# A graph network kernel: batch-norm moments gathered inside the SpMM, in six chunks instead of five

## The reference

```python
def _sage_mean(h, src, dst, W_self, W_neigh, b):
    msg_sum = jax.ops.segment_sum(h[src], dst, num_segments=N_NODES)
    deg = jax.ops.segment_sum(jnp.ones_like(dst, jnp.float32), dst, num_segments=N_NODES)
    h_neigh = msg_sum / jnp.maximum(deg, 1.0)[:, None]
    return h @ W_self.T + h_neigh @ W_neigh.T + b

def _bn(h, gamma, beta):
    mu = jnp.mean(h, axis=0)
    var = jnp.mean(jnp.square(h - mu), axis=0)
    return (h - mu) * jax.lax.rsqrt(var + EPS) * gamma + beta
```

## Time and profile before

| | |
|---|---|
| median of 3 runs | 2182.11 us (2176.29 to 2182.74) |
| the profiled execution | 2189.64 us |
| its span, first to last instruction | 2187.5 us |
| mean granted TensorE clock, share of full speed | 0.923 |
| PE busy | 1743.2 us, 80% |
| DVE busy | 1493.0 us, 68% |
| ACT busy | 1128.8 us, 52% |
| POOL busy | 905.5 us, 41% |

### The profile page before, as it was taken

The page is one execution under the profiler, slowest core; times in us unless marked ns, Lnnn a source line. Parts: engine busy times, 40 slices in busy tenths (PEclk is TensorE's granted clock), DMA queues, the critical chain, the costliest instruction groups (busy, mean ns, idle before and its releaser), DMA issues. The chain is left out here.

```text
span 2187.5 us, 36919 instructions
## 1 busy us (share of the span) xinstructions
PE 1743.2 (80%) x9939; PEld 887.8 (41%) x9940; DVE 1493.0 (68%) x4029; ACT 1128.8 (52%) x2234; POOL 905.5 (41%) x833
## 2 busy tenths in 40 slices
PE   2777776882688878888887888779998998999776
PEld 0222222551344434444443444465535544553444
DVE  6999997434456556566555665478887887888554
ACT  5777776112333333333333333348886886888311
POOL 1000000005666666666666666325553554555300
PEclk9999999996899999898999998879999999999877
DMA  6000000102111111111111111230000000000000
GB/s 174 0 0 0 0 0 15 58 13 53 31 31 29 30 29 30 33 29 30 30 30 30 29 30 30 47 76 1 1 0 1 1 1 1 1 1 1 15 1 15
DMA packets 29632, 50.73 MB, mean 23 GB/s; under 512 B 12820, under 2 KB 13826, under 8 KB 29054
## 3 DMA queue, kind: packets, MB, share of 16 engines
q0 software_dynamic: 17664, 18.12, 4.8%
q1 hardware_dynamic: 11890, 31.59, 4.7%
HBM read 36.58 MB, written 7.39 MB: 20 GB/s over the span
## 5 line engine op out<-in xcount | busy, mean ns | idle before, releaser
L821 POOL DMA_INDIRECT adj<-h_table,l_idx x544 | 557.3, 1024 | 318.9 <-issue 150.2
L1011 DVE TENSOR_SCALAR adj<-adj,node_key 125x1024 f16<-125x1024 f16 x825 | 372.8, 495 | 357.6 <-PE psum L956 159.7
L956 PE MATMUL psum<-adj,x_sb 125*128 125x512 f16 x1650 | 438.7, 407 | 149.1 <-DVE adj L1011 131.0
L1569 POOL TENSOR_TENSOR gat_ring<-gat_ring,adj 125x750 f32<-125x750 f32 (+2 forms) x225 | 311.0, 1384 | 267.1 <-ACT gat_ring L1623 265.0
L1464 DVE SCALAR_TENSOR_TENSOR gat_ring<-x_sb,gat_node,psum 125x750 f32<-125x750 f32 (+2 forms) x375 | 317.9, 861 | 62.1 <-PE psum L1700 26.3
L884 ACT ACTIVATE l_z<-psum 128x320 f32<-128x320 f32 x204 | 89.1, 437 | 478.9 <-remote 250.9
L956 PEld LDWEIGHTS psum<-adj,x_sb 125*128 125x128 f16 x1650 | 161.4, 103 | 359.3 <-DVE adj L1011 172.2
L387 PE MATMUL psum<-col_hot,src_hot 128*128 128x500 bf16 x808 | 206.2, 377 | 110.4 <-DVE src_hot L316 89.8
L1697 PE MATMUL psum<-gat_ring,gat_hx 125*65 125x500 f32 (+1 forms) x500 | 244.2, 578 | 17.3 <-DVE gat_ring L1475 9.5
L313 DVE TENSOR_SCALAR col_hot<-iota_h,c_tab 128x500 bf16<-128x500 f16 x808 | 227.7, 346 | 25.4 <-PE psum L387 20.8
L1620 ACT ACTIVATE gat_ring<-gat_ring,gat_node 125x750 f32<-125x750 f32 (+2 forms) x225 | 182.2, 810 | 61.2 <-DVE gat_ring L1464 59.4
(11 more groups left out here) (243 smaller groups left out, 2177.5 us busy)
## 6 DMA issues: line engine op xcount, KB each, us to landing
adj<-h_table,l_idx POOLq DMA_INDIRECT x544
adj<-key_table SPq DMA_DIRECT2D x33, 250.0 KB
adj<-adj SPq DMA_DIRECT2D x3, 1662.5 KB
adj_saved<-adj SPq DMA_DIRECT2D x1, 3840.3 KB
adj<-adj_saved SPq DMA_DIRECT2D x5, 688.2 KB
x_sb<-in_x SPq DMA_DIRECT2D x1, 781.2 KB
x_saved<-x_sb SPq DMA_DIRECT2D x1, 781.2 KB
out<-x_sb SPq DMA_DIRECT2D x5, 156.2 KB
```

Source lines behind the costliest of these rows:

```text
L821: pool.indirect_dma_start(out=to[:, t, :], out_offset=None, in_=table[:, :], in_offset=bass.IndirectOffsetOnAxis(ap=index[:, t:t + 1], axi ...
L956: last = pe.matmul(psum[:, PAIR[half] + t, :], h_parts[:, k, :], select[0:P, k % SELECTS, t * GE:(t + 1) * GE], start=(k == 0), stop=(k == ...
L1011: v.tensor_scalar(select[0:P, k % SELECTS, :], keys, node_key[:, k:k + 1], None, ALU.is_equal).then_inc(s_sel, 1)
L1569: pool.tensor_tensor(slot, slot, adj[:, k, cols(c)], ALU.mult).then_inc(s["weight_ready"], 1)
```

## The change

The SpMM runs in six chunks of 5, 5, 5, 5, 3 and 2 tiles, in all four layers. TensorE's transposes of chunk c and its projection of chunk c - 1 are issued among the 25 steps of chunk c (after steps 5 and 11; in the last chunk after 9 and 20; in the first chunk the transposes after step 21). VectorE runs `read(c)` after `join(c)`, and no more one chunk later.

In L3 the block `batch_norm_lrelu` is gone. The mean of the first chunk (a matmul with ones in chunk 1, after step 22) is subtracted from the first chunk, and from the bias of all others. ScalarE squares each chunk in the layer itself, VectorE sums values and squares (`both`), and TensorE adds both at the end with six matmuls over 128 columns (`add_moments`). Mean, variance, one gain and one offset per feature follow in small instructions at the end of the layer; the bound is formed during the first chunk. Gain, offset and leaky relu are applied by chunks: for the first batch norm at the start of l3b, in front of the fp16 split, for the second in a last block, where VectorE adds the residual too, and GpSimd nothing.

```diff
+SCHUNK = (5, 5, 5, 5, 3, 2)
+SC = len(SCHUNK)
+SSTART = [sum(SCHUNK[:c]) for c in range(SC)]
+assert sum(SCHUNK) == NT and max(SCHUNK) == TC
+BOUND_AT = 22
+TURN_AT, PROJECT_SAGE_AT = (5,) * (SC - 1) + (9,), (11,) * (SC - 1) + (20,)
...
-        def sage_layer(tag, h, stack, high, parts, scale, z, bias, w, mean, after_chunk=None, column_sums=None, loops=None):
+        REFERENCE, TOTALS = slice(0, D), slice(0, 2 * D)
+
+        def sage_layer(tag, h, stack, high, parts, affine, z, bias, w, mean, after_chunk=None, moments=None, loops=None):
...
+                            link(v.tensor_tensor(zc, pa, over_features(inv_deg[:, tiles], n), ALU.mult))
+                            v.tensor_tensor(zc, zc, over_tiles(bias if moments is None or c == 0 else shifted_bias, n), ALU.add)\
+                                .then_inc(s_zc, 1)
...
+                            by_feature = zc.rearrange("p t d -> p d t")
+                            if c == 0:
+                                v.tensor_reduce(both[:, 0, 0, :], by_feature, AX.X, ALU.add).then_inc(s_sums, 1)
+                                dve.wait_ge(s_ref, 1)
+                                link(v.tensor_scalar(bn[:, 0, :], psum[0:P, 5, REFERENCE], 1.0 / (n * P), None, ALU.mult))
+                                link(v.tensor_tensor(shifted_bias, bias, bn[:, 0, :], ALU.subtract))
+                                link(v.tensor_tensor(zc, zc, over_tiles(bn[:, 0, :], n), ALU.subtract))
+                            v.tensor_reduce(both[:, c, 0, :], by_feature, AX.X, ALU.add).then_inc(s_sums, 1)
...
+                    def square_sums(c):
+                        dve.wait_ge(s_squared, c + 1)
+                        v.tensor_reduce(both[:, c, 1, :], h[:, groups[c], :].rearrange("p t d -> p d t"), AX.X, ALU.add)\
+                            .then_inc(s_both, 1)
+
+                    def low(c, scaled):
+                        tiles = chunks[c]
+                        dve.wait_ge(s_high, c + 1)
+                        v.scalar_tensor_tensor(parts[:, tiles, D:2 * D], parts[:, tiles, 0:D], -LO_SCALE, scaled[:, tiles, :],
+                                               ALU.mult, ALU.add).then_inc(s_split, 1)
+
+                    def gained(c):
+                        tiles = chunks[c]
+                        v.tensor_tensor(z[:, tiles, :], z[:, tiles, :], over_tiles(affine[0], TC), ALU.mult).then_inc(s_gained, 1)
+
+                    def moved(c):
+                        tiles = chunks[c]
+                        dve.wait_ge(s_gained, c + 1)
...
+                    def bent(c):
+                        zc = z[:, chunks[c], :]
+                        dve.wait_ge(s_scaled, c + 1)
+                        v.scalar_tensor_tensor(h[:, chunks[c], :], zc, 0.01, zc, ALU.mult, ALU.max).then_inc(s_bent, 1)
...
+                    if affine is None:
+                        for c, tiles in enumerate(chunks):
                             link(v.tensor_scalar(z[:, tiles, :], h[:, tiles, :], LO_SCALE, None, ALU.mult))
...
-                        else:
-                            v.scalar_tensor_tensor(z[:, tiles, :], h[:, tiles, :], LO_SCALE, over_tiles(scale, TC),
-                                                   ALU.mult, ALU.mult).then_inc(s_scaled, 1)
...
+                            low(c, z)
+                    else:
+                        for c in range(NC):
+                            gained(c)
+                            moved(c)
+                            if c >= 1:
+                                low(c - 1, h)
+                            bent(c)
+                        low(NC - 1, h)
...
-                    for c in range(NC):
+                    if moments is not None and bounds is not None:
+                        gamma, beta, b0, b1 = moments["gamma"], moments["beta"], bounds["bound"][:, 0, :], bounds["bound"][:, 1, :]
+                        link(v.scalar_tensor_tensor(b0, gamma, -1.0, gamma, ALU.mult, ALU.max))
+                        link(v.scalar_tensor_tensor(b1, beta, -1.0, beta, ALU.mult, ALU.max))
+                        link(v.scalar_tensor_tensor(b0, b0, float(int(N ** 0.5) + 1), b1, ALU.mult, ALU.add))
+                        link(v.tensor_scalar(b0, b0, 1e-30, None, ALU.max))
+                        v.tensor_scalar(b1, b0, 1.0 / LO_SCALE, None, ALU.mult).then_inc(s_bound, 1)
+                        link(v.reciprocal(bn[:, 0, :], b0))
...
+                        dve.wait_ge(s_col, 1)
+                        link(v.tensor_copy(bounds["column"], psum[:, 5, 0:1]))
+                        link(v.tensor_scalar(bounds["w"], bounds["w"], bounds["column"], None, ALU.mult))
+                    for c in range(SC):
                         join(c)
-                        if c >= 1:
-                            read(c - 1)
-                    read(NC - 1)
-                    dve.wait_ge(s_zc, NC)
-                    if column_sums is not None:
-                        dve.wait_ge(s_sums, NC)
+                        if moments is not None and c >= 1:
+                            square_sums(c - 1)
+                        read(c)
+                    dve.wait_ge(s_zc, SC)
+                    if moments is not None:
+                        square_sums(SC - 1)
+                        mean_of, var_of, work = bn[:, 0, :], bn[:, 1, :], bn[:, 2, :]
+                        dve.wait_ge(s_total, 1)
+                        link(v.tensor_scalar(bn[:, 0:2, :].rearrange("p k d -> p (k d)"), psum[0:P, 7, TOTALS], 1.0 / N, None, ALU.mult))
+                        link(v.tensor_tensor(work, mean_of, mean_of, ALU.mult))
+                        link(v.tensor_tensor(var_of, var_of, work, ALU.subtract))
+                        v.tensor_scalar(var_of, var_of, 0.0, LN_EPS, ALU.max, ALU.add).then_inc(s_var, 1)
+                        dve.wait_ge(s_std, 1)
+                        link(v.reciprocal(work, work))
+                        link(v.tensor_tensor(moments["gain"], moments["gain"], work, ALU.mult))
+                        link(v.tensor_tensor(work, mean_of, moments["gain"], ALU.mult))
+                        link(v.tensor_tensor(moments["offset"], moments["offset"], work, ALU.subtract))
...
+                        if affine is None:
                             act.activation(parts[:, tiles, 0:D], h[:, tiles, :], ACT.Copy).then_inc(s_high, 1)
                         else:
-                            act.wait_ge(s_scaled, c + 1)
-                            act.activation(parts[:, tiles, 0:D], z[:, tiles, :], ACT.Copy,
+                            act.wait_ge(s_bent, c + 1)
+                            act.activation(parts[:, tiles, 0:D], h[:, tiles, :], ACT.Copy,
...
+                    def squares(c):
+                        if c == 0:
+                            act.wait_ge(s_sums, 2)
+                        act.wait_ge(s_zc, c + 1)
+                        act.activation(h[:, groups[c], :], z[:, groups[c], :], ACT.Square).then_inc(s_squared, 1)
+
+                    for c, n in enumerate(SCHUNK):
+                        act.wait_ge(s_t, c + 1)
+                        if c >= 2:
+                            act.wait_ge(s_z, c - 1)
+                        act.activation(by_tile(stack[D:2 * D, c % 2, 0:n * P]), blocks(3)[0:D, 0:n, 0:P], ACT.Copy)\
+                            .then_inc(s_self, 1)
                         act.wait_ge(s_agg, c + 1)
                         if c >= 2:
                             act.wait_ge(s_rows, c - 1)
-                        act.activation(by_tile(high[:, c % 2, :]), blocks(c % 2)[0:D, 0:TC, 0:P], ACT.Copy).then_inc(s_out, 1)
-                        act.wait_ge(s_t, c + 1)
-                        if c >= 2:
-                            act.wait_ge(s_z, c - 1)
-                        act.activation(by_tile(stack[D:2 * D, c % 2, :]), blocks(3)[0:D, 0:TC, 0:P], ACT.Copy).then_inc(s_self, 1)
+                        act.activation(by_tile(high[:, c % 2, 0:n * P]), blocks(c % 2)[0:D, 0:n, 0:P], ACT.Copy).then_inc(s_out, 1)
+                        if moments is not None and c >= 1:
+                            squares(c - 1)
+                    if moments is not None:
+                        squares(SC - 1)
+                        act.wait_ge(s_var, 1)
+                        act.activation(bn[:, 2, :], bn[:, 1, :], ACT.Sqrt).then_inc(s_std, 1)
...
+                    def spmm(c, steps):
+                        n, first = SCHUNK[c], SSTART[c] * P
+                        near = min(n, 4)
+                        if steps.start == 0:
+                            if c >= 2:
...
+                        for k in steps:
...
+                            last = pe.matmul(o[:, 0:near, 0:P], parts[:, k, :], by_tile(adj[:, k, first:first + near * P]),
+                                             start=(k == 0), stop=(k == NT - 1), skip_group_check=True)
+                            if n > near:
```

(92 more changed lines are left out.)

167 lines of the change are left out of this document (40 added, 127 removed).

## The result

| | before | after |
|---|---|---|
| median of 5 runs each, same chip | 2182.51 us | 2166.04 us (2161.01 to 2166.85) |
| ratio | | 0.9923, 95% interval 0.9903 to 0.9944 |
| the profiled execution, its span | 2189.64, 2187.5 us | 2166.85, 2165.1 us |
| mean granted TensorE clock | 0.923 | 0.937 |
| PE busy | 1743.2 us | 1718.9 us |

The account below looks back on a forecast made before the run. TensorE was taken to bound the SpMMs, and engines waiting in turn the two batch norms of L3. A gain of 18.4 less 0.7 in L0, 17.7 us off 2182.11, gave 2164.4 us, range 2158 to 2171.

Parts of the forecast that it names:

- moments to offset: Small instructions at each L3 layer's end: 1.39 us as before plus 1.36 for five added ones, 2.75 us.
- l3b's SpMM: The second SpMM of L3: 40.66 us before, 2.36 and 0.23 more after the change.
- last block, to its last addition: Final block of the kernel: 20 VectorE instructions take 8.7 us, where it took 10.45 before.
- L0: Layer without batch norm: l0b 0.7 us worse (4.4 instead of 3.7), l0a even (5.8 against 5.7).
- End of the SpMM: In l3a, 2.36 us of TensorE's work moves ahead of the end, 0.35 is added; 250-column matmuls take 0.107 us.
- Tail: From the SpMM's end to the moments in L3: 4.3 us, with 3.7 and 4.9 as ends.
- Restart: Start of l3b: first low part after 2.9 us, then chunks every 1.8; first matmul 11.1 us earlier.
- Rival B: Waited chunk instructions start every 0.52 instead of 0.42 us, and loads bound 250-column matmuls: 2170 us; chance 12%.
- End: Last addition to the span's end takes 3.8 us as before, stores every 1.7 us without queueing; end 18.4 us earlier.
- Moved and free: Work moved beside the SpMM costs nothing: about 3 us of bound instructions, join(1) some 0.8 us later.
- A: Small fp32 pieces leave holes in the SpMM, TensorE falls to 1.2 GHz, 6.7 us per five-tile chunk: 2191; chance 4%.
- C: The serial tail doesn't shrink because some wait holds until the end: gain below 6 us, 2177; chance 4%.

Follow-up runs that it names:

- e4: Changed kernel with each of the five result stores issued as two, over 112 and 13 partitions: L3 127.7 against 131.9 us, span ends 2.47 us after the last addition.
- e6: Changed kernel with the last block's residual added by GpSimd again: L3 132.5 against 131.9 us.
- e7: Changed kernel with matmuls of ones behind l3a's moments and before l3b's first step: l3b's first join at 9.44 instead of 10.51 us, L3 130.4.
- e9: Changed kernel with split stores and matmuls of ones in all layers, against the kernel before: 2020.93 against 2040.66 us, ratio 0.9901, on another chip.
- e8: Changed kernel with l3b's gain, offset and leaky relu over all 25 tiles instead of by chunks: L3 134.8 against 131.9 us.
- e11: Kernel before with each result store issued as two, over 112 and 13 partitions: end after the last addition 2.46 instead of 3.78 us.
- e10: Changed kernel with squares and their sums taken behind the last projection instead of during the SpMM: L3 137.8 against 131.9 us.
- e1: Six chunks and interleaved issue, but the old batch norm, against the kernel before: 2181.74 against 2180.64 us, ratio 1.0008.
- e5: Changed kernel with transposes and projection so early in each chunk that TensorE waits for join: L3 140.2 against 131.9 us, execution 2181.64 us.
- e2: Changed kernel with five chunks of five tiles instead of six: L3 133.4 against 131.9 us, L0 111.5 against 110.0.
- e3: Changed kernel with transposes and projections at each chunk's end instead of among its steps: L3 131.4 against 131.9 us.

## Why the prediction was right, step by step

| step | predicted | measured |
|---|---|---|
| l3a's SpMM, first step to last | 43.5 | 43.50 |
| its end to the moments read (L616) | 4.3 (3.7 to 4.9) | 4.22 |
| moments to offset | 2.75 | 2.68 |
| block's start to l3b's first matmul | 2.9 | 2.93 |
| l3b's SpMM | 43.25 | 43.74 |
| last block, to its last addition | 8.7 | 8.38 |
| last addition to the span's end | 3.8 | 5.06 |
| L3, gain | 18.4 | 17.2 |
| L0, loss | 0.7 | 0.1 |

The forecast held in L3 because the serial stretch was counted instruction by instruction; in L0 it held by luck. Its terms:

- *End of the SpMM.* 2.36 us of work moved in and 0.35 added gave 43.5, and after had 43.50. This is partly luck: the same SpMM took 42.39 to 43.50 in the executions of e4, e6, e7, e9 and after, so the term was some 0.5 too long. That 250 columns take 0.107 us held: eleven loads in 1.18 us (L672). The count lacked the 0.05 us per pair of joints inside a chunk.
- *Tail.* Right in size, and wrong in why. I took a value between full and half clock. The clock stayed at 1.00, and the ten early moment loads hid; VectorE's own work with its hand-offs took 4.2 and not 3.7. Taken at full clock, the step would have been 0.5 too short.
- *Restart.* The instructions start every 0.40, as the earlier trace rows promised with 0.42, also where each waits for one two before it. Rival B's 0.52 was seen only at the dependent pair at either end of the block. The Trainium skill, VectorE: DVE Perf Modes, section on the TRN2 errata, advises 512 elements or more; 320 were the better size here, by 3.3 us in L3 (e8), since chunking let TensorE begin.
- *l3b's SpMM.* Nine steps ran at half clock (0.50 to 2105.2) where I had seven: 0.5 us.
- *End.* The step that was wrong is "3.8 as before; the timeline gives no sign that one waits for another". I had looked for stores that wait in before, and there are none; what I didn't do is hold a store's own length against the new pace. The DMA view of before has it: mostly 79 to 126 GB/s between the dips, which is 1.3 to 2.0 us for 160 KB, no safe distance from 1.7. I also gave all five additions one pace, but only one instruction lies between the last two, and they end 0.93 us apart. The queue costs 1.3 us, and e4 and e11 show it from both sides.
- *L0.* Luck. l0b ends 0.86 later from its own start (0.7 predicted) and l0a takes 0.27 more up to the norm's loads (even predicted), but the norm block between them was 0.95 shorter, since more of its 18 matmul loads ran at the high clock. The change doesn't explain that. First the row of after, then that of before:

```profile
435.07 2.95 PEld L417 LDWEIGHTS psum<-ones 128*128 128x128 f32 x18 [1.89 <-issue]
```

```profile
435.78 3.92 PEld L411 LDWEIGHTS psum<-ones 128*128 128x128 f32 x18 [3.15 <-issue]
```

  And the same rows of e10, whose L0 is the code of after, and of e11, whose L0 is that of before:

```profile
435.66 3.91 PEld L417 LDWEIGHTS psum<-ones 128*128 128x128 f32 x18 [1.94 <-issue]
```

```profile
434.90 3.17 PEld L411 LDWEIGHTS psum<-ones 128*128 128x128 f32 x18 [3.15 <-issue]
```

  Either code has had either length, so this 0.95 is one execution against another. By parts at equal clock L0 loses about 1.0 us: 0.27 in l0a, 0.53 up to l0b's first join (8.27 against 7.74 in l0a, where the clock is up in both) and 0.24 behind it. e1 has the same 1.0.

- *Moved and free.* `join(1)` of l3a comes 9.07 us after `join(0)`, where e1 has 8.39: the 0.7 that I put at 0.8. Nobody waited for it; `join(2)` is back in step.
- *Rivals.* A's place was real, and its price wrong: a wait of 0.88 us lengthens a five-tile chunk by 0.8 (9.15 against 8.38) and not by 6.7 (e5). The least slack, in the three-tile chunk, held, and no projection inside after's SpMM waits. C fell: tail and chain shrank as counted.

What L3 loses when one part of the change is taken away, with the clock taken out: moments inside the SpMM 6.3 us (e10), affine by chunks 3.3 (e8), a short last chunk 2.9 (e2), residual on VectorE 0.9 (e6), interleaving 0.4 (e3). These are prices within the changed kernel, and not all are shares of the 17.2: the 2.9 is measured against five chunks with the pieces among the steps, a worse order than that of before, and e1 gives the whole schedule 1.0 us at most. With 1.0 for it, 5 to 6 us are left (an estimate) for the fewer serial steps: one round of sums over TensorE instead of two, no centring, no bound in the chain, one block less. They weren't taken apart, and the parts needn't add up. Also not tried is a feed of l3b by ScalarE as well as VectorE, which e7 says binds next.

## What to carry to other kernels

When a serial stretch is made shorter, hold the new pace of its producer against each queue behind it: a store that took 1.86 us was hidden at one per 1.99 and not at one per 1.61, and least of all where the last piece came 0.93 us behind the one before it. Statistics that can be gathered beside the bound engine (here sums and squares about the first chunk's mean) are worth more than any finer interleaving of that engine's own work, which only moves it. And compare stages rather than spans: two executions of unchanged code differed by more than most parts of this change.
